# A pipelined attention kernel: TensorE sums the weighted rows of a chunk two chunks behind its exponentials instead of one

## The reference, cut to what matters

```python
b, s, _ = x.shape                                   # 4 x 1024 tokens, 256 wide
Q = (x @ Wq + bq).reshape(b, s, H, C) * inv_sqrt_c  # H, C = 16, 64
K = (x @ Wk + bk).reshape(b, s, H, C)
V = (x @ Wv + bv).reshape(b, s, H, C)
scores = jnp.einsum('bshq,bshk->bshqk', Q, K)       # for each token and head: 64 x 64 outer product
scores = jnp.where(mask, -inf, scores)              # channel q sees channels k <= q
w = jax.nn.softmax(scores, axis=-1)
attn = jnp.einsum('bshqk,bshk->bshq', w, V)
x = x + attn.reshape(b, s, HID) @ Wo + bo + down(silu(gate(x)) * up(x))
```

## Time and profile before

| | |
|---|---|
| runs, us | 4469.23, 4469.39, 4474.24; median 4469.39 |
| profiled execution, us | 4464.44 (span of its core 4462.7) |
| PE busy | 3698.7 us, 83% of the span |
| POOL busy | 3553.5 us, 80% |
| DVE busy | 3338.4 us, 75% |
| ACT busy | 1973.1 us, 44% |
| mean granted TensorE clock | 0.923 of full speed |

### The profile page before, as it was taken

The page is one execution under the profiler, slowest core; times in us unless marked ns, Lnnn a source line. Parts: engine busy times, 40 slices in busy tenths (PEclk is TensorE's granted clock), DMA queues, the critical chain, the costliest instruction groups (busy, mean ns, idle before and its releaser), DMA issues.

```text
span 4462.7 us, 78596 instructions
## 1 busy us (share of the span) xinstructions
PE 3698.7 (83%) x27777; PEld 3258.2 (73%) x27777; DVE 3338.4 (75%) x3762; ACT 1973.1 (44%) x2564; POOL 3553.5 (80%) x1935
## 2 busy tenths in 40 slices
PE   4115779993017999999999999999999999999999
PEld 3003368872006888888888888888888898888888
DVE  8702343333557898899898889889889989889987
ACT  1001023331004555555555555555555555555555
POOL 1774045556767999999999999999999999999997
PEclk8557889996558999999999999999999999999999
DMA  9221089997340000000000000000000000000000
GB/s 351 73 96 57 0 314 360 366 357 247 98 139 3 7 5 5 5 5 6 7 6 5 5 5 6 5 7 5 5 5 5 6 7 5 5 5 5 6 7 5
DMA packets 154902, 291.38 MB, mean 65 GB/s; under 512 B 22608, under 2 KB 116048, under 8 KB 154576
## 3 DMA queue, kind: packets, MB, share of 16 engines
q0 software_dynamic: 38912, 151.04, 9.6%
q1 hardware_dynamic: 115664, 135.80, 8.7%
HBM read 181.77 MB, written 104.99 MB: 64 GB/s over the span
## 4 chain that ended last, share of the span: by engine, by line
POOL 36%; issue 28%; PE 4%; DVE 1%; ACT 0%; POOLq 0%; DMA 0%; ACTq 0%; DVEq 0%
POOL at_s L1083 32%; POOL at_m L1067 2%; POOL at_fall L1063 2%; PE at_den L1299 1%; PE at_num L1299 1%; POOL at_m L1060 1%; PE at_work L1271 0%; PE at_work L1276 0%; DVE at_pv L1199 0%; POOLq L1082 0%; PE at_misc L1329 0%; DVE at_s L1191 0%; PE at_work L1287 0%; ACT at_s L1154 0%; PE at_misc L1323 0%
## 5 line engine op out<-in xcount | busy, mean ns | idle before, releaser
L1083 POOL TENSOR_TENSOR at_s<-at_s,at_m 128x2048 f32<-128x2048 f32 (+15 forms) x1024 | 2549.5, 2527 | 117.1 <-DVE at_s L1191 116.4
L1154 ACT ACTIVATE at_s<-at_s 128x2048 f32<-128x2048 f32 (+15 forms) x1024 | 1135.6, 1112 | 1259.0 <-POOL at_s L1083 1253.6
L1191 DVE TENSOR_TENSOR at_s<-at_q,at_kp 128x2048 f32<-128x2048 f32 (+15 forms) x1024 | 1311.8, 1281 | 325.3 <-PE at_den L1299 308.2
L1299 PE MATMUL at_den<-k_ident,at_s 128*128 128x128 f32 x10240 | 1291.9, 273 | 55.5 <-ACT at_s L1154 55.5
L1199 DVE TENSOR_TENSOR at_pv<-at_s,at_vp 128x2048 f32<-128x2048 f32 (+15 forms) x1024 | 1312.4, 1282 | 15.6 <-ACT at_s L1154 3.5
L1299 PE MATMUL at_num<-k_ident,at_pv 128*128 128x128 f32 x10240 | 1285.9, 273 | 0.0
L1299 PEld LDWEIGHTS at_num<-k_ident,at_pv 128*128 128x128 f32 x10240 | 1162.0, 141 | 145.6 <-issue 123.3
L1299 PEld LDWEIGHTS at_den<-k_ident,at_s 128*128 128x128 f32 x10240 | 1158.0, 141 | 80.1 <-ACT at_s L1154 62.1
L648 POOL DMA_INDIRECT moe_w<-experts,e_weight_row x256 | 242.2, 946 | 342.4 <-PE moe_yp L675 159.9
L138 POOL DMA_INDIRECT slot_x<-e_xn,e_slot x192 | 206.1, 1074 | 152.0 <-DVE e_slot L358 87.6
L668 PE MATMUL moe_gu<-moe_xT,moe_w 128*128 128x128 f32 x2048 | 277.5, 279 | 14.9 <-issue 8.9
(11 more groups left out here) (219 smaller groups left out, 3349.5 us busy)
## 6 DMA issues: line engine op xcount, KB each, us to landing
slot_x<-k_region SPq DMA_DIRECT2D x16, 2048.0 KB, 22.9
moe_x<-slot_x SPq DMA_DIRECT2D x256, 128.0 KB
slot_out<-moe_yo SPq DMA_DIRECT2D x256, 128.0 KB
xT<-cmb_xT SPq DMA_DIRECT2D x33, 128.0 KB
at_xT<-xT SPq DMA_DIRECT2D x33, 128.0 KB, 2.0
e_x<-u SPq DMA_DIRECT2D x4, 1024.0 KB, 10.9
moe_w<-experts,e_weight_row POOLq DMA_INDIRECT x256
x<-e_x SPq DMA_DIRECT2D x4, 1024.0 KB
```

Of the source, the lines that this page charges most:

```text
L1083: nc.gpsimd.tensor_tensor(part(s_all, c), part(s_all, c), by_query(m[h][:], c), ALU.subtract).then_inc(sub_done, 1)
L1154: nc.scalar.activation(part(s_all, c), part(s_all, c), ACT.Exp, scale=C ** -0.5).then_inc(exp_done, 1)
L1191: v.tensor_tensor(part(s_all, c), by_query(q[h][:], c), by_key(kp[:], c), ALU.mult).then_inc(mult_done, 1)
L1299: ins = nc.tensor.matmul(dst[:, b * P:(b + 1) * P], buf[:, at:at + P], k.ident[:], start=(x == 0 and b == 0), stop=False, is_transpose=Tru ...
```

## The change

Each num is issued one chunk later in TensorE's order: at chunk c TensorE sums the weighted rows of chunk c - 2 instead of c - 1, and the last two chunks of a unit are summed in the next unit. No instruction is added or removed, and the other engines' programs are the same.

```diff
@@ -922,6 +922,7 @@
 LAG = 3
+BEHIND = 2
@@ -1371,10 +1372,10 @@
                             up(u, r, s)
-                        if c:
-                            sum_num(n, h, c - 1)
+                        if c >= BEHIND:
+                            sum_num(n, h, c - BEHIND)
                         elif not (first(t) and h == 0):
-                            sum_num(n - 1, 1 - h, NCH - 1)
+                            sum_num(n - 1, 1 - h, NCH + c - BEHIND)
@@ -1388,7 +1389,8 @@
                 unit_loop(pe, unit)
-                sum_num(2 * NT - 1, 1, NCH - 1)
+                for c in range(NCH - BEHIND, NCH):
+                    sum_num(2 * NT - 1, 1, c)
```

## The result

The changed kernel takes 4550.0 us (median of four, 4548.6 to 4556.4) against 4469.3 us before; the ratio is 1.0185, 95% interval 1.0172 to 1.0198. The change costs about 81 us. The forecast was 4548 us, with a range of 4503 to 4570. (The changed kernel's trace is of its longest execution, 4556.4 us: 92 us more than the traced one of before. 9.5 us of that lie ahead of the first tile's Q_low, almost all of it in the first layer, which the change doesn't touch.)

A forecast was written before the change was run, and what follows sets the result against it. TensorE's stretch from Q_low to den(10) of h = 1 was taken to bound the tile. 4469.4 us plus 41.5 for the longer stretch and end and 37.2 for clock falls gave 4548 us, range 4503 to 4570.

The forecast's parts named there:

- The bound: TensorE's gapless stretch from Q_low to den(10) of h = 1, then the chain back to Q_low, sets a tile's time.
- the change's net twelve: Between Q_low and den(10): num(0) adds 16 transposes, num(8) takes off 4; 1.31 us a tile, 40.6 us over 31.
- The gap: TensorE's idle time before Q_low grows from 1.28 to 2.59 us a tile; the one before den(0) stays.
- The falls: Granted clock falls behind the longer gap before Q_low: 22 of 31 tiles at 1.69 us, 37.2 us.
- all 31 tiles would fall: Upper case by the skill page's rule: a clock fall in every tile, 52.4 us, 4563 us in total.
- The cover at tv(7): VectorE stands about 1.7 us at tv(7) for num(3) in units with h = 0; GpSimd's slack makes it cost nothing.
- The wait of the weight loads for pv: Sign in the new trace: TensorE's weight loads no longer wait for the weighted rows, 7.2 us before.
- The clock stays up: Rival 1: no falls behind Q_low's gap, only the 1.31 us a tile; 4511 us; chance 0.26.
- Faster, by 0.44 us a tile: Rival 2: den(10) of each second unit reached num(8) sooner, 13.5 us in all, 4456 us; chance 0.06.

The follow-up runs named there:

- sixteen transposes in: Kernel before, with num(0) of each unit with h = 0 moved from ahead of Q_low to behind it; ratio 1.0262.
- four out: Changed kernel, with num(0) of each unit with h = 0 taken back to right ahead of Q_low; ratio 0.9970.
- both ends moved: Kernel before, with num(1) of h = 0 right ahead of Q_low and num(7), num(8) of h = 1 behind den(10); ratio 0.9894.
- twelve fillers: Changed kernel, with twelve identity transposes that compute nothing used added ahead of Q_low in units with h = 0; ratio 1.0111.
- six fillers: Changed kernel, with six identity transposes that compute nothing used added ahead of Q_low in units with h = 0; ratio 1.0155.
- num(1) alone: Kernel before, with num(1) of each unit with h = 0 issued right ahead of Q_low instead of right behind it; ratio 0.9887.
- three places: Kernel before, num(1) of h = 0 ahead of Q_low; in h = 1 num(7), num(8) behind den(10), num(2) behind the Q projection's second half; ratio 0.9901.

## Why the prediction was right

**The bound.** That TensorE's stretch from Q_low to den(10) sets the tile holds: sixteen transposes in, 1.74 us more without a fall; four out, 0.46 less; the change's net twelve, 1.29 us (1.31 forecast). That den(10) is where the stretch ends is half the story: for a shift that lengthens, the latest way decides, and it is that of den(10); where that way alone is shortened, another binds, the gate product in the trace with both ends moved.

**The gap.** 2.59 us before Q_low, as forecast, and the one before den(0) unchanged.

**The falls.** Their price, 1.69 us, measured 1.67; their number was a choice, 22 of 31, and is 28. The errors of the whole sum are that term, 6 x 1.69 = 10 us too few, and the three falls of the kernel before that I didn't take off, 5 us too many: for both reasons together the forecast should have lain 5 us off, and it lay 2 us off. So the nearness of 4548 to 4550 is in part luck. With 28 - 3 the sum is 41.5 + 42.3 = 83.8 us, ratio 1.0187 against 1.0185 measured. The rows behind the 22 seemed to divide at a gap of 2.0 us; that wasn't a limit, for in the changed kernel gaps of 2.10 and 2.07 us before den(0) brought no fall.

The prediction took from the Trainium skill, page "TensorE: Matmul & The Clock Gate", section "HAM oscillation — how this bites in real kernels", that all 31 tiles would fall. The kernel described there waits 3 to 5 us in every pass, longer than the 2.59 us here, so the page doesn't settle this case. The trace shows 28 of 31, nearer to all than my 22.

**The cover at tv(7).** VectorE's wait for num came up, but not in the place and size forecast: at tv(7) of units with h = 0 it is 1.30 us (at 2991.28) instead of 1.7, and with the other four it is 4.6 us a tile (138.6 us in 30 tiles). GpSimd's wait came with it. They cost nothing: the version that keeps them but takes num(0) back is faster than the kernel before.

**A sign that failed.** The wait of the weight loads for pv was to be gone. It is 9.9 us from 1500 to 4490, against 7.2 before. It is 0.3 us a tile and bears on nothing, but the delayed nums didn't remove it.

**The rivals.** "The clock stays up" is a true kernel, the one with twelve fillers, at 1.0111. "Faster, by 0.44 us a tile" is true of the change without num(0).

## What to carry to other kernels

When an order is changed on the engine that bounds a kernel, don't ask what each instruction waits for, but on which side of that engine's own gaps it stands. Here work ahead of a gap was free until the gap was full; the same work behind it was paid in full, however patient its reader. Waits of the other engines that grow by hundreds of microseconds can cost nothing, and a gap of two microseconds on TensorE can cost twice, the second time through its clock. Count the falls in the trace, and look whether a later wait of TensorE's takes them up. If a gap can't be avoided, fill it, best with work that has to be done anyway, as num(1) here; the fillers here spoiled the output, and none that don't were tried.

## What the runs showed of the hardware

The length of a gap alone doesn't decide whether the clock falls, though the count grows with it (0, 20, 25 and 28 of 31 above). In the kernel before a gap of 1.94 us didn't bring it down, with six fillers 20 of 31 gaps of 1.94 did, and with twelve fillers a gap as long as 2.31 us before den(0) was followed by a clock of 1.00. Rows of TensorE's timeline and of a 4 us stretch from that last kernel:

```profile
3528.88 1.97 PE L1300 MATMUL at_den<-k_ident,at_s 128*128 128x128 f32 x16 [2.31 <-ACT at_s L1155]
...
3529.00:3533.00 4.00, 4.00 (x25) 2.88 (x26) 3.78 (x3) 2.15 (x3) 4.00 (x2) 1.00 0.02 4
```

With six fillers the gap of 1.94 us stands behind the same instructions in every tile, and 11 of them kept the clock up. So neither the length nor the work just ahead decides by itself. That it is where in time the gap lies is an inference; no run here moved a gap in time and nothing else. Two orders with the same tile without falls can so differ by some falls, as the traces with num(1) alone (3 falls), with both ends moved (9) and with three places (2, in the 30 tiles from the second on) do. Their ratios, 0.9887, 0.9894 and 0.9901, have overlapping intervals, so no rank among them is shown.
